# The last block of an attention-and-feed-forward layer: square sums by a ones column, statistics of two tiles on ScalarE, the predecessor's tiles shared

## The reference, cut

```python
x = x + attention(x)        # 8 x 1024 tokens of 256 channels, 16 heads, linear attention with softmaxes
x = layernorm(x)            # "x1" below
h = layer_norm(x, g1, b1)
h = gelu(h @ ternary(w1).T + b1)           # hidden 1024
h = layer_norm(h, g2, b2)
y = h @ ternary(w2).T + b2
out = layernorm(x + y)      # mean and variance over the 256 channels of a token
```

## Time and profile before

| | us |
|---|---|
| median of 3 runs | 551.71 (551.33 to 552.11) |
| the profiled execution, its own time | 551.79 |
| its span, first to last instruction | 549.9 |
| granted TensorE clock over the span | 0.994 |

### The profile page before, as it was taken

One profiled execution on the slowest core, in us unless ns is written; L12 is line 12 of the kernel. 1 busy time (PEld: TensorE's weight loads), 2 busy tenths in 40 slices (PEclk: granted clock), 3 DMA queues, 4 the chain that ended last, 5 costly groups with the idle time before them and its releaser, 6 DMA issues.

```text
span 549.9 us, 10913 instructions
## 1 busy us (share of the span) xinstructions
PE 532.1 (97%) x3541; PEld 492.0 (89%) x3541; DVE 481.8 (88%) x1227; ACT 478.6 (87%) x952; POOL 414.7 (75%) x429
## 2 busy tenths in 40 slices
PE   8999999999999999989999999999999999999993
PEld 7999999898999989879987999999999999999992
DVE  5888998989899898878788899999999999999896
ACT  5745789798978878778799999999999999999996
POOL 2965969877796986478468878888888877776782
PEclk9999999999999999999999999999999999999997
DMA  8530050320705021070011003322125253010012
GB/s 337 203 122 1 1 230 2 131 100 11 297 1 229 2 87 69 1 266 5 0 40 41 1 0 117 117 76 79 50 68 116 78 93 94 34 53 38 39 40 114
DMA packets 12679, 46.51 MB, mean 85 GB/s; under 512 B 1360, under 2 KB 3792, under 8 KB 10448
## 3 DMA queue, kind: packets, MB, share of 16 engines
q1 hardware_dynamic: 12336, 45.28, 23.7%
q10 hardware_dynamic: 288, 0.54, 0.3%
HBM read 29.01 MB, written 16.81 MB: 83 GB/s over the span
## 4 chain that ended last, share of the span: by engine, by line
PE 68%; ACT 11%; DVE 11%; POOL 5%; issue 3%; DMA 2%; SPq 0%; POOLq 0%; DVEq 0%; ACTq 0%
PE ring L2005 19%; PE qps_sps_aps_then_y L2027 19%; PE qps_sps_aps_then_y L1787 5%; PE qps_sps_aps_then_y L1893 5%; PE qps_sps_aps_then_y L1873 5%; PE ring L1815 5%; DVE z L1285 3%; PE ring L1945 2%; POOL xt_lo L462 2%; PE ring L1920 1%; PE ring L1908 1%; PE ring L1960 1%; ACT ek L745 1%; DMA xc<-in_x_first_dram 1%; POOL ff_accp_over_xt_lo L588 1%
## 5 line engine op out<-in xcount | busy, mean ns | idle before, releaser
L2027 PE MATMUL qps_sps_aps_then_y<-ff_w_over_xc_lo,ff_a_lo_over_qw 128*128 128x258 f32 x512 | 126.5, 283 | 0.0
L2027 PE MATMUL qps_sps_aps_then_y<-ff_w_over_xc_lo,ff_a_hi_over_xc_lo 128*128 128x258 f32 x512 | 126.4, 283 | 0.0
L1367 DVE SCALAR_TENSOR_TENSOR ff_a_lo_over_qw<-ring,ff_rho,ff_a_hi_over_xc_lo 128x512 fp32r<-128x512 f32 x128 | 92.8, 743 | 12.5 <-ACT ff_a_hi_over_xc_lo L881 11.4
L2005 PE MATMUL ring<-ff_ht_hi_over_qw,t 128*128 128x512 f32 x256 | 103.7, 405 | 0.1
L2005 PE MATMUL ring<-ff_ht_lo_over_xc_hi,t 128*128 128x512 f32 x256 | 100.5, 393 | 0.0
L2027 PEld LDWEIGHTS qps_sps_aps_then_y<-ff_w_over_xc_lo,ff_a_lo_over_qw 128*128 128x128 f32 x512 | 96.8, 189 | 3.3
L2027 PEld LDWEIGHTS qps_sps_aps_then_y<-ff_w_over_xc_lo,ff_a_hi_over_xc_lo 128*128 128x128 f32 x512 | 96.7, 189 | 3.4
L863 ACT ACTIVATE ring<-ring,bias 128x512 f32<-128x512 f32 x128 | 84.5, 689 | 6.7 <-PE ring L2005 5.5
L588 POOL TENSOR_TENSOR ff_accp_over_xt_lo<-ff_accp_over_xt_lo,ff_sq_over_ek_et_hi 128x512 f32<-128x512 f32 x66 | 86.0, 1303 | 2.0
L879 ACT ACTIVATE ff_sq_over_ek_et_hi<-ring 128x512 f32<-128x512 f32 x128 | 80.5, 629 | 0.5
L881 ACT CAST ff_a_hi_over_xc_lo<-ring 128x512 fp32r<-128x512 f32 x128 | 79.5, 621 | 0.0
(11 more groups left out here) (200 smaller groups left out, 1615.4 us busy)
## 6 DMA issues: line engine op xcount, KB each, us to landing
...
```

The costliest lines, as they stand in the source:

```text
L1367: nc.vector.scalar_tensor_tensor(out=ff_a_lo[:, m % DEPTH], in0=ff_bank(k, m), scalar=ff_rho[:, m:m + 1], in1=ff_a_hi[:, m % DEPTH].bitcas ...
L2005: mm = nc.tensor.matmul(ff_bank(k, m), t1[:, c, m * P:(m + 1) * P], h[:, k % 2, c], start=(c == 0 and j == 0), stop=(c == CH - 1 and j == 1))
L2027: last = nc.tensor.matmul(ff_yps[:, t, 0:C + 2], a[:, m % DEPTH, t * P:(t + 1) * P], ff_w2[:, m], start=(m == 0 and j == 0), stop=(m == FC ...
```

## The change

It touches the end of the lists alone.

- Squares: GpSimd adds chunks 1 to 5 only. VectorE adds chunks 6 and 7 and then both sums (two operations of 128x512). TensorE multiplies each 128 tokens of the total by one column of `ones` (`last_square_sums`), which puts a token's sum on its partition, and `last_hidden_variance` reads that column straight from PSUM; transposes and reduce fall away. The four columns lie in the bank that held the transposes.
- The last block's rows lie in `ff_xn` (free by then: the rows of the last transposes), not in `ff_z[:, 1]`, so no residual waits for block 13's store.
- Statistics of tiles 0 and 1: the residual also gives the row's sum (`l_sum`), VectorE makes the negative means, and ScalarE squares the centred row with its sum (`last_squares`) and takes the root. Tiles 2 and 3 keep `bn_stats` and `bn_aggr`.
- Block 14's statistics are spread between the steps of block 15; its root is on ScalarE instead of GpSimd's power, its inverse and shift are `previous_shift` on VectorE, and its tiles are normalised by ScalarE (tile 0) and GpSimd (tiles 1 to 3). Its store waits for both.
- The normalising of block 15: ScalarE has tiles 0 and 2, VectorE tiles 1 and 3.

The diff, without the names of tiles and semaphores:

```diff
@@ -386,7 +389,11 @@
-                sp.wait_ge(ff_o_ok, TB * (k + 1))
+                if k == NK - 2:
+                    sp.wait_ge(l_act, 1)
+                    sp.wait_ge(l_prev_ok, TB - 1)
+                else:
+                    sp.wait_ge(ff_o_ok, TB * (k + 1))
@@ -430,9 +437,8 @@
-                if g == 1:
-                    sp.wait_ge(l_dve, 1)
-                sp.dma_start(out[NB - 1, :, T - TB + 2 * g:T - TB + 2 * g + 2], ff_z[:, (NK - 1) % 2, 2 * g:2 * g + 2]
+                sp.wait_ge(l_dve, g + 1)
+                sp.dma_start(out[NB - 1, :, T - TB + 2 * g:T - TB + 2 * g + 2], ff_xn[:, 2 * g:2 * g + 2]
@@ -687,10 +693,12 @@
-            for m in range(5, FC):
-                ff_square_sum(NK - 1, m)
-            ff_out_rstd(NK - 2)
+            ff_square_sum(NK - 1, 5)
...
+            pool.wait_ge(ff_z_nmr, NK - 1)
+            for t in range(1, TB):
+                nc.gpsimd.tensor_scalar(ff_z[:, NK % 2, t], ff_z[:, NK % 2, t], ff_rsZ[:, t:t + 1], ff_nmr[:, t:t + 1],
+                                        ALU.mult, ALU.add).then_inc(l_prev_ok, 1)
@@ -1114,25 +1122,33 @@
+                if t == TB - 1:
+                    act.wait_ge(ff_r_eps, NK)
+                    nc.scalar.activation(l_root[:, 0], ff_var[:], ACT.Sqrt).then_inc(l_two_roots, 1)
...
-            act.wait_ge(ff_r_eps, NK)
-            nc.scalar.activation(l_root[:, 0], ff_var[:], ACT.Sqrt).then_inc(l_hidden_root, 1)
-            ff_normalise_out(NK - 2, (0, 1, 2, 3))
-            def last_root(g):
-                act.wait_ge(ff_z_var, TB * (NK - 1) + 2 * g + 2)
-                nc.scalar.activation(l_root[:, 1, 2 * g:2 * g + 2], l_mv[:, 2 * g:2 * g + 2, 1], ACT.Sqrt, bias=eps[:, 0:1]
-                                     ).then_inc(l_root_ok, 1)
+            def last_squares():
+                act.wait_ge(l_mean, 1)
+                for t in range(2):
+                    nc.scalar.activation(ff_yc[:, t], ff_xn[:, t], ACT.Square, bias=l_nm[:, t:t + 1],
+                                         accum_out=l_ss[:, t:t + 1]).then_inc(l_sq, 1)
...
-                nc.scalar.activation(ff_z[:, (NK - 1) % 2, n], ff_z[:, (NK - 1) % 2, n], ACT.Identity,
+                nc.scalar.activation(ff_xn[:, n], ff_xn[:, n], ACT.Identity,
...
-            last_root(0)
+            act.wait_ge(ff_z_var, TB * (NK - 1))
+            nc.scalar.activation(l_prev_root[:], ff_mvZ[:, :, 1], ACT.Sqrt, bias=eps[:, 0:1]).then_inc(l_two_roots, 1)
+            last_squares()
+            act.wait_ge(l_sq, 2)
+            nc.scalar.activation(l_root[:, 1, 0:2], l_ss[:], ACT.Sqrt, bias=eps[:, 0:1], scale=1.0 / C).then_inc(l_root_ok, 1)
+            act.wait_ge(ff_z_nmr, NK - 1)
+            nc.scalar.activation(ff_z[:, NK % 2, 0], ff_z[:, NK % 2, 0], ACT.Identity, bias=ff_nmr[:, 0:1],
+                                 scale=ff_rsZ[:, 0:1]).then_inc(l_act, 1)
...
-            last_normalise(1)
-            last_root(1)
+            act.wait_ge(ff_z_var, TB * (NK - 1) + 2)
+            nc.scalar.activation(l_root[:, 1, 2:4], l_mv[:, 2:4, 1], ACT.Sqrt, bias=eps[:, 0:1]).then_inc(l_root_ok, 1)
@@ -1444,33 +1461,51 @@
-                dve.wait_ge(l_hidden_root, 1)
+                dve.wait_ge(l_two_roots, 1)
...
-                nc.vector.reciprocal(ff_rsH[:], l_root[:, 0]).then_inc(l_hidden_inv, 1)
-            def last_residual(ts):
-                dve.wait_ge(l_hidden_inv, 1)
-                wait_for(dve, ff_o_out[(NK - 1) % 2], 16 * ((NK - 1) // 2))
-                for t in ts:
-                    dve.wait_ge(l_centred, t + 1)
-                    dve.wait_ge(ff_x1c_ok, PIECES * (NK - 1) + t * PIECES // TB + 1)
-                    nc.vector.scalar_tensor_tensor(
-                        out=ff_z[:, (NK - 1) % 2, t], in0=ff_yps[:, t, 0:C], scalar=ff_rsH[:, t:t + 1],
-                        in1=ff_x1c[:, (NK - 1) % 2, t], op0=ALU.mult, op1=ALU.add).then_inc(ff_z_ok, 1)
-            def last_variance(g):
-                dve.wait_ge(ff_z_stat, TB * (NK - 1) + 2 * g + 2)
-                nc.vector.memset(fence[:], 0.0)
-                for n in range(2 * g, 2 * g + 2):
-                    nc.vector.bn_aggr(l_mv[:, n], ff_bnZ[:, n]).then_inc(ff_z_var, 1)
-            def last_shift(g):
+                nc.vector.reciprocal(ff_rsH[:], l_root[:, 0]).then_inc(l_two_inverses, 1)
+            def last_hidden_variance():
+                dve.wait_ge(ff_r_tr, NK)
+                dve.wait_ge(ff_r_sq, NK)
+                nc.vector.scalar_tensor_tensor(out=ff_var[:], in0=ff_sum_bank(NK - 1)[:, 0:TB], scalar=1.0 / F,
+                                               in1=ff_msq[:], op0=ALU.mult, op1=ALU.subtract).then_inc(ff_r_var, 1)
+                dve.wait_ge(ff_r_var, NK)
+                nc.vector.tensor_scalar(ff_var[:], ff_var[:], 0.0, EPS, ALU.max, ALU.add).then_inc(ff_r_eps, 1)
+            def last_residual(t):
+                if t == 0:
+                    dve.wait_ge(l_two_inverses, 1)
+                    dve.wait_ge(ff_ht_tr, CH * NK)
+                dve.wait_ge(l_centred, t + 1)
+                dve.wait_ge(ff_x1c_ok, PIECES * (NK - 1) + t * PIECES // TB + 1)
+                total = {"accum_out": l_sum[:, t:t + 1]} if t < 2 else {}
+                nc.vector.scalar_tensor_tensor(
+                    out=ff_xn[:, t], in0=ff_yps[:, t, 0:C], scalar=ff_rsH[:, t:t + 1],
+                    in1=ff_x1c[:, (NK - 1) % 2, t], op0=ALU.mult, op1=ALU.add, **total).then_inc(ff_z_ok, 1)
+            def previous_shift():
+                dve.wait_ge(l_two_roots, 2)
+                nc.vector.reciprocal(ff_rsZ[:], l_prev_root[:]).then_inc(l_two_inverses, 1)
+                dve.wait_ge(l_two_inverses, 2)
+                dve.wait_ge(ff_o_ok, TB * (NK - 2))
+                nc.vector.scalar_tensor_tensor(out=ff_nmr[:], in0=ff_mvZ[:, :, 0], scalar=-1.0, in1=ff_rsZ[:],
+                                               op0=ALU.mult, op1=ALU.mult).then_inc(ff_z_nmr, 1)
+            def last_means():
+                dve.wait_ge(ff_z_ok, TB * (NK - 1) + 2)
+                nc.vector.tensor_scalar(l_nm[:], l_sum[:], -1.0 / C, None, ALU.mult).then_inc(l_mean, 1)
+            def last_inverse(g):
...
-                nc.vector.scalar_tensor_tensor(out=l_shift[:, ts], in0=l_mv[:, ts, 0], scalar=-1.0, in1=l_rs[:, ts],
-                                               op0=ALU.mult, op1=ALU.mult).then_inc(l_nmr, 1)
+            def last_normalise(t):
+                dve.wait_ge(l_nmr, t // 2 + 1)
+                nc.vector.tensor_scalar(ff_xn[:, t], ff_xn[:, t], l_rs[:, t:t + 1],
+                                        l_shift[:, t:t + 1], ALU.mult, ALU.add).then_inc(l_dve, 1)
@@ -1689,24 +1724,34 @@
-            ff_out_stats(NK - 2, (0, 1))
-            ff_out_stats(NK - 2, (2, 3))
+            ff_square_sum(NK - 1, 7)
+            ff_square_total(NK - 1)
+            ff_out_stats(NK - 2, (0,))
+            ff_hidden_mean(NK - 1)
+            ff_out_stats(NK - 2, (1,))
+            last_hidden_variance()
+            ff_out_stats(NK - 2, (2,))
+            last_hidden_inverse()
+            last_residual(0)
+            ff_out_stats(NK - 2, (3,))
...
-            ff_hidden_mean(NK - 1)
-            ff_hidden_stats(NK - 1)
-            ff_out_shift(NK - 2)
-            last_hidden_inverse()
-            last_residual((0, 1))
-            ff_out_stats(NK - 1, (0, 1))
-            last_variance(0)
-            last_residual((2, 3))
-            last_shift(0)
+            last_residual(1)
+            last_means()
+            previous_shift()
+            last_residual(2)
+            last_residual(3)
...
-            last_variance(1)
-            last_shift(1)
-            dve.wait_ge(l_nmr, 2)
-            nc.vector.tensor_scalar(ff_z[:, (NK - 1) % 2, 3], ff_z[:, (NK - 1) % 2, 3], l_rs[:, 3:4], l_shift[:, 3:4],
-                                    ALU.mult, ALU.add).then_inc(l_dve, 1)
+            last_inverse(0)
+            nc.vector.tensor_tensor(l_shift[:, 0:2], l_nm[:], l_rs[:, 0:2], ALU.mult).then_inc(l_nmr, 1)
+            dve.wait_ge(ff_z_stat, TB * NK - 2)
+            nc.vector.memset(fence[:], 0.0)
+            for t in (2, 3):
+                nc.vector.bn_aggr(l_mv[:, t], ff_bnZ[:, t]).then_inc(ff_z_var, 1)
+            last_normalise(1)
+            last_inverse(1)
+            nc.vector.scalar_tensor_tensor(out=l_shift[:, 2:4], in0=l_mv[:, 2:4, 0], scalar=-1.0, in1=l_rs[:, 2:4],
+                                           op0=ALU.mult, op1=ALU.mult).then_inc(l_nmr, 1)
+            last_normalise(3)
@@ -1947,18 +1992,21 @@
-                if not 0 <= k < NK:
-                    return
-                if k < NK - 1:
-                    pe.wait_ge(ff_sum_d, D_ADDS * (k + 1))
-                    ff_bank_free(k + 1, 1)
-                else:
-                    pe.wait_ge(ff_sum_p, P_ADDS * k + FC - 1)
-                    ff_bank_free(k, 5)
-                acc = ff_accd if k < NK - 1 else ff_accp
+                if not 0 <= k < NK - 1:
```

(13 more changed lines are left out.)

16 lines of the change are left out of this document (10 added, 6 removed).

## The result

| | before | after |
|---|---|---|
| median of 20 runs each, us | 551.73 (551.33 to 552.26) | 552.68 (552.33 to 552.99) |
| ratio | | 1.0016, 95% interval 1.0009 to 1.0023 |
| the profiled execution, us | 551.79 | 552.99 |
| its span, us | 549.9 | 551.1 |

Forecast were 551.0 us and a range up to 551.9: the time lies outside the range, on the other side of before. The computing of the tail was shortened by more than the sum said, and time was lost in two places, in the blocks before it and in the last stores, that the sum did not contain.

The account below looks back on a forecast made before the run. From 538.5 us no engine is full, so a chain of waits bounds the tail: 1.40 us won to the first residual less 0.65 given back takes 0.75 from 551.79, giving 551.04, written 551.0; range 550.4 to 551.9.

Parts of the forecast that it names:

- All is unchanged until VectorE is free at 536.78: Everything ahead of the tail: instructions before 536.78 us were taken to keep their times from the old trace.
- the steady part moves: Rival: five small tiles shift SBUF addresses behind them, zero to one us either way around 551.0; chance 0.06.
- The ones column: TensorE's token sums in the last block: eight records, 1.1 us, 538.25 to 539.34, so variance starts at 539.45.
- the short chain: Rival: ones product done by 538.6, variance 0.39 us earlier, 0.15 more if the shift misses GpSimd; 550.5, chance 0.16.
- the slow column: Rival: eight records at 0.22 us or a late VectorE sum, variance 0.8 us later; 551.5, chance 0.12.
- To the first residual: Last block, variance through inverse root: first residual starts at 540.31 instead of 541.71, 1.40 us earlier.
- What is given back: First residual to last normalise, with block 14's leftovers on VectorE: 0.65 us of the 1.40 won is lost.
- the hold of the first shift behind GpSimd: First pair's shift on VectorE, two SBUF inputs: waits from 544.06 until GpSimd's tiles end at 544.2.
- The hold on the residuals: Rival: GpSimd's normalising holds the last block's residuals, 1.4 us later; 552.4, or 553 with a statistic; chance 0.06.
- Nothing is lost, and nothing is in hand: Last stores at 400 GB/s: the last 256 KB may flow from 547.0, just when its own issue lets it.
- GpSimd holds the stores: Rival: GpSimd's tiles take 0.8 us, not 0.55, delaying block 14's store and the last half by 0.75; 551.8, chance 0.12.

Follow-up runs that it names:

- e1: The changed kernel with its four new small tiles allocated behind all others, no instruction different; ratio to the kernel before 0.9989.
- e2: The kernel before with four unused 32-byte tiles added, all behind them 128 bytes higher, no instruction different; ratio to before 1.0023.

## Why the prediction was wrong, step by step

- **"All is unchanged until VectorE is free at 536.78": the step that failed.** The first sentence of the sum held the instructions fixed and took their times as fixed too. They cost 1.4 us more over the blocks, because the four new tiles moved their operands (e1, e2). The rival "the steady part moves" named exactly this, "zero to one us either way", with a chance of 0.06: the mechanism was on the list, its size was set too small and its chance far too low.
- **The ones column: right.** Eight records in 0.95 us, 0.11 apart from the second on; 1.1 us forecast. The variance waited 0.15 us for it and started 3.22 us behind the last `ff_act_low`; forecast 539.45 - 536.12 = 3.33. Neither *the short chain* nor *the slow column*.
- **To the first residual: right.** 1.45 us earlier for 1.40.
- **What is given back: too high by 0.2 us.** From first residual to the last normalise's end 5.69 us (547.76 - 542.07); forecast 5.88 (546.19 - 540.31), before 5.23. Much of the difference is the hold of the first shift behind GpSimd, 0.15 us in the sum and 0.02 in the trace: the product of two SBUF tiles took 0.18 us at 545.73, and the second shift, of the same size, takes 0.16 where GpSimd is idle (546.96). The hold was real, and its end was mis-sized. In all eleven traces with this product it took 0.178 to 0.195 us, always ending 0.003 to 0.006 us behind the end that GpSimd's third tile is drawn with (545.90 in after). The residuals from `ff_yc` that the additions hold show the same in before: seven of them took 0.79 to 1.51 us instead of 0.48, and each ended 0.28 us behind the addition. So the hold ends about 0.16 to 0.2 us ahead of GpSimd's drawn end (an estimate from these rows), and the sum let the shift wait for the drawn end itself. The Trainium skill, "SBUF — State Buffer", section "SBUF: two separate sides", would have the later one wait for the end of the whole instruction that it meets. The trace agrees on the wait, not on the drawn end as its measure: from 545.90 the product would have ended at 546.06.
- **The hold on the residuals: no.** The two at 544.09 took 0.88 us, the second of them beside GpSimd's first tile; two took 0.88 without it before.
- **"Nothing is lost, and nothing is in hand" in the stores: the second step that failed.** The issue times were right to 0.3 us, counted from the last `ff_act_low`: block 14's store at 8.05 us (forecast 8.12), the last half at 9.85 (10.10). The rate was not: 400 GB/s was read from the middle slices of a single store. From its first packet to its last, block 14's store took 1.44 us in before (365 GB/s) where the sum had 1.3, a half 0.83 where it had 0.65, and the three in a row 3.0 in after where it had 2.6. With nothing in hand, each 0.1 us of that showed. The rival *GpSimd holds the stores* had the place, the last half behind block 14's store, and the size within a factor of two, but another cause: GpSimd took 0.54 us for a tile, as forecast.

The tail as a whole brought 1.0 - 0.4 = 0.6 us, 0.75 forecast. Without the moved tiles (e1) the change is 0.11% faster than before, 0.13% forecast.
